# State space model in a four-part network on Trainium2: GpSimd multiplies every fourth state by C, and the states have four buffers

## The reference

```
u, z   = silu(conv(in_proj(x)))[128, 1024], silu(in_proj_z(x))[128, 1024]
dt, Bm, Cm = split(W_x @ u)              # 4, 16 and 16 rows
delta  = softplus(W_dt @ dt + b_dt)      # [128, 1024]
for n in range(16):                      # the 16 states
    h_n[t] = exp(delta[t] * A[:, n]) * h_n[t-1] + (delta[t] * u[t]) * Bm[n, t]
y[t]   = sum over n of h_n[t] * Cm[n, t]   +  u[t] * Dp
out    = W_out @ (y * z) + x
```

## Time and profile before

| what | us |
|---|---|
| median of 3 runs (lowest to highest) | 3701.83 (3694.66 to 3702.51) |
| the profiled execution | 3700.42 |
| its span, first to last instruction | 3698.7 |
| of the span: from the gate product of the first image to that of the last | 1034.32 |

### The profile page before, as it was taken

How to read it: one execution, slowest core, us unless ns; L and a number is a source line. 1 busy time by engine, 2 the same in 40 slices (tenths; PEclk the granted TensorE clock), 3 DMA queues, 4 the chain that set the end, 5 groups by cost and what they waited for, 6 DMA issues and landing times. The chain is left out here.

```text
span 3698.7 us, 55733 instructions
## 1 busy us (share of the span) xinstructions
PE 3182.4 (86%) x18550; PEld 1189.8 (32%) x18550; DVE 2573.7 (70%) x3346; ACT 2006.4 (54%) x2381; POOL 2214.9 (60%) x684
## 2 busy tenths in 40 slices
PE   6999999999999999999996899764888888888887
PEld 2333333333333333333332233341322322322322
DVE  5777777777777777777772222132888888988988
ACT  3566666566666666666664333223555564564564
POOL 0577777777777777777778000002666666666666
PEclk7899999999999999999998999885999999999999
DMA  2000000000000000000002311123333443443443
GB/s 102 12 16 11 15 16 16 16 10 18 16 16 10 16 16 16 16 11 16 18 10 43 122 68 45 37 75 130 135 133 125 154 139 118 154 146 111 154 147 116
DMA packets 74760, 235.10 MB, mean 64 GB/s; under 512 B 13088, under 2 KB 14180, under 8 KB 74420
## 3 DMA queue, kind: packets, MB, share of 16 engines
q1 hardware_dynamic: 69460, 215.06, 17.1%
q0 software_dynamic: 5056, 16.83, 1.3%
HBM read 192.42 MB, written 39.39 MB: 63 GB/s over the span
## 5 line engine op out<-in xcount | busy, mean ns | idle before, releaser
L526 DVE TENSOR_REDUCE at_pmax<-at_ring 128x1 f32<-128x512 f32 x2048 | 1301.1, 685 | 416.4 <-PE at_ring L334 405.5
L479 ACT ACTIVATE at_probs<-at_sc 128x1024 f32<-128x1024 f32 x1024 | 992.6, 1021 | 559.9 <-PE at_sc L402 557.2
L580 POOL TENSOR_TENSOR at_prob_sums<-at_prob_sums,at_probs 128x2048 f32<-128x2048 f32 x256 | 1159.1, 4528 | 74.8 <-ACT at_probs L479 54.7
L398 PE MATMUL at_sc<-at_QT,at_KT 32*128 32x512 f32 x4096 | 782.9, 638 | 22.4 <-issue 22.0
L1634 POOL TENSOR_TENSOR ss_drive<-ss_du,ss_bsb 128x1024 f32<-128x1024 f32 x261 | 611.0, 2354 | 270.6 <-DVE ss_state L1591 263.0
L1534 ACT ACTIVATE ss_decay<-ss_delta,ss_a 128x512 f32<-128x512 f32 x520 | 354.5, 687 | 447.2 <-DVE ss_state L1587 301.3
L410 PE MATMUL at_O<-at_probs,at_V 128*32 128x512 f32 x4096 | 538.7, 610 | 52.5 <-DVE at_att L549 51.7
L580 POOL TENSOR_TENSOR at_prob_sums<-at_probs 128x2048 f32<-128x2048 f32 x64 | 290.9, 4545 | 432.3 <-ACT at_probs L479 432.3
L1423 PE MATMUL ss_Y<-ss_seen,ss_ident 128*128 128x512 f32 x1032 | 524.0, 632 | 0.0
L334 PE MATMUL at_ring<-at_KH,at_QH 32*128 32x512 bf16 x2048 | 442.8, 389 | 5.7 <-DVE at_pmax L526 2.9
L1599 DVE TENSOR_TENSOR ss_seen<-ss_state,ss_C 128x1024 f32<-128x1024 f32 x259 | 316.2, 1221 | 87.7 <-PE ss_C L1411 79.8
(11 more groups left out here) (199 smaller groups left out, 2699.4 us busy)
## 6 DMA issues: line engine op xcount, KB each, us to landing
ss_bsb<-scratch_rows SPq DMA_DIRECT2D x265, 512.0 KB, 7.0
scratch_attn<-at_att SPq DMA_DIRECT2D x64, 256.0 KB, 2.0
fc_att<-scratch_attn SPq DMA_DIRECT2D x32, 512.0 KB, 5.8
ss_xn<-scratch_xm SPq DMA_DIRECT2D x34, 256.0 KB, 5.7
at_xn<-scratch_xn SPq DMA_DIRECT2D x32, 256.0 KB, 3.9
ss_xw<-scratch_xw SPq DMA_DIRECT2D x17, 256.0 KB, 3.9
ln_x<-in_x SPq DMA_DIRECT2D x8, 512.0 KB, 4.2
scratch_xn<-ln_xn POOLq DMA_DIRECT2D x8, 512.0 KB, 3.0
```

What stands on the lines that cost most here:

```text
L398: nc.tensor.matmul(sc[:, h, :], KT[head(h), par, blk(kb)], QT[head(h), par, hs(half)], start=True, stop=False)
L479: nc.scalar.activation(probs[:, kb, two, :].rearrange("p h q -> p (h q)"), sc[:, two, :].rearrange("p h q -> p (h q)"), ACT.Exp, scale=SCA ...
L526: nc.vector.tensor_reduce(pmax[:, quad // 2, h, quad % 2:quad % 2 + 1], ring[:, unit[3], :], AX_X, ALU.max, negate=True).then_inc(max_done, 1)
L580: nc.gpsimd.tensor_tensor(prob_sums[:, half, :, :], before, probs[:, k, :, :], ALU.add).then_inc(pool_sums, 1)
```

## The change

- GpSimd makes the product with C for the states 1, 5, 9 and 13 (`of_pool`), in step n, behind the drive of n + 2. VectorE and TensorE's spread of C leave these states out. Accumulation of such a state waits for GpSimd's product (`pool_seen`).
- The C rows of these states reach GpSimd by DMA. ScalarE's copy takes 32 rows of B and C instead of 16 rows of B (`rows`, 128 KB per image in the scratch), and SyncE issues a 512 KB spread of row 16 + n behind that of B, six states ahead, into two places (`csb`). Ahead of it, it waits until the product of two such states before is done.
- The states have four buffers instead of two. VectorE waits, ahead of the scan of such a state, for the product of the one before.
- The counts of `seen_done` go by the twelve states that VectorE still multiplies.

```diff
+    TURN_OF_POOL = 1
...
-        brow = sb("ss_brow", [N, 2, S])
+        rows = sb("ss_rows", [2 * N, 2, S])
+        csb = sb("ss_csb", [P, 2, S])
...
-        state = sb("ss_state", [P, 2, S])
+        state = sb("ss_state", [P, DEPTH, S])
...
+        c_in = [sem(f"ss_c_in{n}") for n in range(2)]
...
+        def of_pool(n):
+            return n % DEPTH == TURN_OF_POOL
+
+        def seen_before(b, n):
+
+            return (DEPTH - 1) * (N // DEPTH * b + n // DEPTH) + n % DEPTH - (n % DEPTH > TURN_OF_POOL)
...
# SyncE
-                sp.dma_start(rows_d[par], brow[:, par, :]).then_inc(rows_out, DMA)
+                sp.dma_start(rows_d[par], rows[:, par, :]).then_inc(rows_out, DMA)
...
                 sp.dma_start(bsb[:, n % SLOTS, :], rows_d[par, n:n + 1, :].broadcast_to([P, S])).then_inc(b_in[n % SLOTS], DMA)
+                if of_pool(n):
+
+                    if not (isinstance(b, int) and b == 0) or n >= 2 * DEPTH:
+                        sp.wait_ge(pool_seen, N // DEPTH * b + n // DEPTH - 1)
+                    place = n // DEPTH % 2
+                    sp.dma_start(csb[:, place, :], rows_d[par, N + n:N + n + 1, :].broadcast_to([P, S])).then_inc(c_in[place], DMA)
...
# TensorE
             def add_state(b, par, n):
-                pe.wait_ge(seen_done, b * N + n + 2)
+                if of_pool(n):
+                    pe.wait_ge(pool_seen, N // DEPTH * b + n // DEPTH + 1)
+                else:
+                    pe.wait_ge(seen_done, seen_before(b, n) + 2)
...
-                pe.wait_ge(seen_done, b * N + n + 1)
-                spread(Cp, N, b, par, n).then_inc(c_ready, 1)
+                if not of_pool(n):
+                    pe.wait_ge(seen_done, seen_before(b, n) + 1)
+                    spread(Cp, N, b, par, n).then_inc(c_ready, 1)
...
# ScalarE
-                nc.scalar.activation(brow[:, par, :], aux[0:N, :], ACT.Copy).then_inc(brow_done, 1)
+                nc.scalar.activation(rows[:, par, :], aux[0:2 * N, :], ACT.Copy).then_inc(brow_done, 1)
...
# VectorE
-                now = state[:, n % 2, :]
+                now = state[:, n % DEPTH, :]
+                if of_pool(n) and not (isinstance(b, int) and b == 0):
+                    dve.wait_ge(pool_seen, N // DEPTH * b + n // DEPTH)
...
             def see(b, par, n):
+                if of_pool(n):
+                    return
                 dve.wait_ge(state_done, b * N + n + 1 + DEPTH)
-                dve.wait_ge(c_ready, b * N + n + 1)
+                dve.wait_ge(c_ready, seen_before(b, n) + 1)
...
# GpSimd
+            def see(b, par, n):
+                pool.wait_ge(c_in[n // DEPTH % 2], (N // DEPTH // 2 * b + n // (2 * DEPTH) + 1) * DMA)
+                pool.wait_ge(state_done, b * N + n + 1 + DEPTH)
+                pool.wait_ge(y_ready, b * N + n + 1)
+                nc.gpsimd.tensor_tensor(seen[:, n % DEPTH, :], state[:, n % DEPTH, :], csb[:, n // DEPTH % 2, :], ALU.mult)\
+                    .then_inc(pool_seen, 1)
+
             def step(b, par, n):
                 make_drive(*ahead(b, par, n, LEAD))
+                if of_pool(n):
+                    see(b, par, n)
...
-        rows_d = scratch("scratch_rows", [2, 16, S])
+        rows_d = scratch("scratch_rows", [2, 32, S])
```

More of the change, by code:

```diff
@@ L1259, in state_space_phase @@
          mid_done, low_done, abs_done, exp_done, soft_done, relu_done, delta_done, du_done, brow_done, rows_out, c_ready,
-         first_half_done, decay_done, drive_done, state_done, seen_done, y_ready, y_step, out_ready, res_done, stored, dt_done) = (
+         first_half_done, decay_done, drive_done, state_done, seen_done, pool_seen, y_ready, y_step, out_ready, res_done, stored, dt_done) = (
             sem(f"ss_{n}") for n in (
@@ L1265, in state_space_phase @@
                 "relu_done", "delta_done", "du_done", "brow_done", "rows_out", "c_ready", "first_half_done", "decay_done", "drive_done",
-                "state_done", "seen_done", "y_ready", "y_step", "out_ready", "res_done", "stored", "dt_done"))
+                "state_done", "seen_done", "pool_seen", "y_ready", "y_step", "out_ready", "res_done", "stored", "dt_done"))
         b_in = [sem(f"ss_b_in{n}") for n in range(SLOTS)]
+        c_in = [sem(f"ss_c_in{n}") for n in range(2)]
         block = ctx.enter_context(nc.Block())
@@ L1363, in _ @@
                 sp.wait_ge(b_slot, 2 * NB * DMA)
+            for place in c_in:
+                sp.wait_ge(place, N // DEPTH // 2 * NB * DMA)
         @block.tensor
@@ L1513, in _ @@
             act.wait_ge(rest_done, 1)
-            nc.scalar.activation(brow[:, 0, :], aux[0:N, :], ACT.Copy).then_inc(brow_done, 1)
+            nc.scalar.activation(rows[:, 0, :], aux[0:2 * N, :], ACT.Copy).then_inc(brow_done, 1)
             middles(0, 0)
@@ L1594, in see @@
             def see(b, par, n):
+                if of_pool(n):
+                    return
                 dve.wait_ge(state_done, b * N + n + 1 + DEPTH)
-                dve.wait_ge(c_ready, b * N + n + 1)
+                dve.wait_ge(c_ready, seen_before(b, n) + 1)
                 dve.wait_ge(y_ready, b * N + n + 1)
-                nc.vector.tensor_tensor(seen[:, n % DEPTH, :], state[:, n % 2, :], Cp[:], ALU.mult).then_inc(seen_done, 1)
+                nc.vector.tensor_tensor(seen[:, n % DEPTH, :], state[:, n % DEPTH, :], Cp[:], ALU.mult).then_inc(seen_done, 1)
             def finish(b, par, n):
```

## The result

The changed kernel is slower: 3712.5 us median of 6 runs (3708.8 to 3719.6) against 3699.8 (3691.3 to 3704.0), a ratio of 1.0042 with a 95% interval of 1.0031 to 1.0054. (All ratios are those on record; they can differ by about 0.1% from the quotient of the two medians, which is 1.0034 here.) Forecast were 3689 us and a gain. The measured time lies at the upper edge of the range, and on the other side of no change.

A forecast was written before the change was run, and what follows sets the result against it. VectorE was taken to set the pace except at three standstills. States 5 and 13 were to save 32.8 us and TensorE's clock to cost 21.5 more, net -11.3 from 3700.4: 3689 us, range 3665 to 3713.

The forecast's parts named there:

- What else moves: Side effects: DMA spreads, larger copy and store, four state buffers, TensorE's new wait; all hidden or 0.
- the prediction's own signs of being wrong: Undisturbed images not 66.0 us, a row spread landing late for the drive, or over 2.9 us per image on the clock.
- State 5, 9, 13, 1: Saving per image by product moved: state 5 1.26 us, 13 0.98 (0.79 after GpSimd's lateness), 9 and 1 nothing.
- Scan after scan, 1.20 us: On VectorE, without a product between, the next first scan starts 1.20 us after the second scan.
- GpSimd: Four more products of 2.35 us, 53.7 us busy per image; hidden, except scan 0 waiting 0.2 us for its drive.
- DMA: Four more 512 KB spreads per image, share 0.49 from 0.40; C rows and queued B rows hidden.
- The clock: TensorE's longer pauses bring second falls: 13 of 16 after the gate product, clock cost 34.7 us, 21.5 added.
- the falls ahead of the projection of u: Without C 9, TensorE's pause there grows from 1.61 to 2.2 us: 8 of 16 falls, 1.2 us each.
- TensorE's spreads: TensorE drops eight matmuls of C, 4 x 0.45 us, on no chain that sets the end; 0.
- The rivals: Clock no worse 0.15, clock eats all 0.14, low twice as long 0.15, GpSimd late 0.05, all four pay 0.06.
- Low twice as long: Rival: TensorE's clock falls in the output chain last 6.8 us, not 3.4; +11 us, 3711; chance 0.15.

The follow-up runs named there:

- e1_counts: Changed kernel, TensorE's count of C spreads raised by 2 behind a GpSimd state, so VectorE waits for b*N+n+1; 3686.1 us, 0.9962 of the kernel before.
- e5: Padded-count version of the changed kernel, with GpSimd making the product for states 5 and 13 alone; 3676.2 us, 0.9938 of the kernel before.
- e6: Padded-count version of the changed kernel, with GpSimd making the product for states 1 and 9 alone; 3707.1 us, 1.0012 of the kernel before.
- e7: e1_counts with the output projection moved behind the spread of C 2 and its result taken one state later; 3691.2 us, 0.9977 of the kernel before.
- e10: e5 with the output projection cut in two, one half ahead of C 2, the other ahead of C 3; 3675.6 us, 0.9926 of the kernel before.
- e9: Changed kernel with VectorE's wait for the spread of C put ahead of its wait for the scan; 3693.0 us, 0.9981 of the kernel before.
- e11: Kernel before, nothing on GpSimd, with the output projection cut in two around C 2; 3671.2 us, 0.9909 of the kernel before.
- e2_before_counts: Kernel before with the count of C spreads rising by 3 each and VectorE waiting for three times the number; 3701.6 us, 0.9997 of the kernel before.

## Why the prediction was wrong

The step that failed is the one that isn't there. "What else moves" prices the DMAs, the copy and TensorE's new wait, and takes the twelve products that stay at the earlier trace rows's 3.80 us per state. They went to about 3.98. Of the prediction's own signs of being wrong one came, undisturbed images that aren't 66.0 us. The diff shows the cause (VectorE waits on `c_ready` for `seen_before(b, n) + 1`), and I read it as bookkeeping. 12 x 0.18 = 2.2 us per image, of which 1.4 come through (67.4 against 66.0 of e1_counts), 15 x 1.4 = 21 us in 15 images. With that term the sum is 3689 + 22 = 3711, near the measured 3712.5, in part by luck: for 15 images it makes 10 us more, and the profiled ones show 6.0, as the clock took less than forecast.

The rest, by its own steps:

- **State 5, 9, 13, 1: right.** 16 x 2.05 = 32.8 us was the sum; undisturbed images of e1_counts are 66.00 us, 66.04 were forecast. The standstills (3.39, 2.25, 2.23) are those of the text (3.4, 2.26, 2.2), and e5 and e6 show each pair by itself.
- **Scan after scan, 1.20 us: right.**
- **GpSimd: right.** 53.2 us per image (53.7), 2349 ns per product. The drive of state 0 is late by 0.2 to 0.4 us in nine images (3.1 us in the phase, the prediction had 0.2 per image).
- **DMA: right for this kernel,** with a share of 0.50 (0.49). The C row never holds a product up. But the input load lands later, 7.1 us from issue instead of 5.7, behind one more spread that is issued just ahead of it, and TensorE waits for it, 3.9 us in the 15 images (10.0 in e1_counts). In e7 and e10 it takes 5.7 and 5.6 us again, and is late because it is issued later.
- **The clock: about right, by a pause that was not the forecast one.** Second falls behind 14 of 16 gate products (13 forecast), after pauses of 2.9 to 3.3 us instead of 2.7; e6, with 2.69 us each time, has 12. The whole clock cost is 29.4 us for 15 images; 34.7 for 16 were forecast. Of the falls ahead of the projection of u, 8 were forecast and 4 came.
- **TensorE's spreads.** A spread of C takes 0.60 us, so four are 2.4 us and not 4 x 0.45. The sum doesn't use it.
- **The rivals.** "Low twice as long" has the right time, 3711, by the wrong mechanism: one fall behind a gate product lasted 6.8 us, the others 3.4. The time coming out as in a rival is no evidence for it.

What stays open: the timed runs differ by 12.8 us, and the profiled ones too, but there 5.9 of these lie ahead of the phase. Over the 14 kernels, one profiled execution of each, the start of the phase moved from 2525.8 to 2535.1 us, so I put no cause to the 6 to 7 us that the images don't show.

## What to carry to other kernels

Ask of each piece of work that is moved what ends the next wait without it: two of the four products here stood under a chain that holds neither, and moving these cost clock and brought nothing. A wait's count is part of the schedule: keep all counts of a loop at the same rate, so that the waiting instruction can take the wait for the engine's own last result itself. Where a count needs a value of its own, write that wait ahead of the one for the last result (e9: 19.5 of the 26 us). Of the engine that has the slack, ask what will be late when the standstill is gone; here the projection was next (e11: 0.9% alone, nothing to be told on top of e5) and then the input load; with both and two products on GpSimd it is 1.5%. The softplus chain is the next, and still stands.

## What the runs showed of the hardware that I had not expected

- On VectorE's sequencer it counts which instruction carries the wait for the engine's own scan. From the start of a scan of 1.28 us to that of the product behind it are 1.32 us with the wait on the product, 1.37 to 1.38 with the wait on a semaphore instruction ahead of it (e9), and 1.47 to 1.50 with the wait on a register operation ahead of both.
- TensorE's clock can lock with a loop. In e2_before_counts 14 images in a row take 68.28 to 68.30 us with one fall of 3.4 us each, while the kernel before, 0.2 us shorter per undisturbed image, wanders between 67.9 and 70.8. 2.6 us more of VectorE's time per image (16 x 0.16) cost nothing there: 0.5 were hidden by two standstills, and 2.0 went with the shorter fall.
